# Attention ahead of an RWKV-style mix on one core: row maxima turned before the V product and the row sums, first scores right behind the sums

## What is computed

```
x = x + attn(layernorm(x))     # 8 heads of 64, softmax over 1024 keys, then W_out, layer norm, (y + x) / sqrt 2
x = x + mix(layernorm(x))      # r = sigmoid(xr W_r), k = xk W_k, out = r * (relu(k)^2 W_v)

qk  = x @ W_qk + b_qk          # q and k of every head, interleaved
v   = x @ W_v + b_v
sim = q k^T * 64^-0.5
o   = softmax(sim) v
```

## Time and profile before

| | |
|---|---|
| median of 3 runs | 2722.21 us |
| profiled execution, own time | 2721.03 us |
| its span | 2719.2 us |
| mean granted TensorE clock | 0.989 |
| TensorE (PE) busy | 2625.8 us, 97% |
| VectorE (DVE) busy | 1631.3 us, 60% |
| ScalarE (ACT) busy | 1290.6 us, 47% |
| GpSimd (POOL) busy | 1521.1 us, 56% |
| idle before ACT's exponentials (L623), ended by PE | 589.6 us |
| idle before DVE's maxima (L417), ended by PE | 543.4 us |

### The profile page before, as it was taken

How to read it: one execution, slowest core, us unless ns; L and a number is a source line. 1 busy time by engine, 2 the same in 40 slices (tenths; PEclk the granted TensorE clock), 3 DMA queues, 4 the chain that set the end, 5 groups by cost and what they waited for, 6 DMA issues and landing times. The chain is left out here.

```text
span 2719.2 us, 31997 instructions
## 1 busy us (share of the span) xinstructions
PE 2625.8 (97%) x11376; PEld 1782.0 (66%) x11376; DVE 1631.3 (60%) x2679; ACT 1290.6 (47%) x1833; POOL 1521.1 (56%) x819
## 2 busy tenths in 40 slices
PE   6999999999999999999999999999579999999999
PEld 5655656665565666556556666665358888888887
DVE  7555455456545545654554555455278787878785
ACT  3345346335534634553463455344245555555554
POOL 3576477567647756764775676577323333333333
PEclk9999999999999999999999999999779999999999
DMA  2222122122112212211221221122322222222220
GB/s 97 63 47 51 36 78 53 42 71 55 44 38 75 55 40 71 57 42 48 66 55 40 70 60 39 40 50 79 122 90 99 85 96 89 93 92 89 96 77 32
DMA packets 108410, 178.32 MB, mean 66 GB/s; under 512 B 22401, under 2 KB 22913, under 8 KB 108289
## 3 DMA queue, kind: packets, MB, share of 16 engines
q1 hardware_dynamic: 108288, 176.75, 22.5%
HBM read 92.02 MB, written 50.59 MB: 52 GB/s over the span
## 5 line engine op out<-in xcount | busy, mean ns | idle before, releaser
L417 DVE TENSOR_REDUCE half_max<-ps_max 128x1 f32<-128x512 f32 x1024 | 680.3, 687 | 549.7 <-PE ps_max L780 543.4
L324 POOL TENSOR_TENSOR acc<-acc,probs 128x1024 f32<-128x1024 f32 x384 | 914.0, 2380 | 157.5 <-ACT probs L623 109.2
L623 ACT ACTIVATE probs<-ps_st 128x1024 f32<-128x1024 f32 x512 | 522.0, 1023 | 591.8 <-PE ps_st L801 589.6
L812 PE MATMUL ps_o<-probs,v 128*64 128x512 f32 x2048 | 467.7, 598 | 0.0
L800 PE MATMUL ps_st<-qA,kA 128*128 128x512 f32 x1024 | 415.3, 406 | 13.9 <-DMA qB<-max_row 9.4
L801 PE MATMUL ps_st<-qB,kB 65*128 65x512 f32 x1024 | 408.2, 399 | 0.0
L780 PE MATMUL ps_max<-kA,qA 128*128 128x512 f32 x1024 | 386.8, 416 | 3.7 <-issue 1.4
L320 POOL TENSOR_TENSOR acc<-probs 128x1024 f32<-128x1024 f32 x64 | 152.8, 2387 | 287.6 <-ACT probs L623 287.6
L812 PEld LDWEIGHTS ps_o<-probs,v 128*64 128x64 f32 x2048 | 135.6, 136 | 265.4 <-issue 236.5
L780 PEld LDWEIGHTS ps_max<-kA,qA 128*128 128x128 f32 x1024 | 188.6, 188 | 138.6 <-issue 63.5
L800 PEld LDWEIGHTS ps_st<-qA,kA 128*128 128x128 f32 x1024 | 194.7, 190 | 82.3 <-ACT probs L623 32.7
(11 more groups left out here) (174 smaller groups left out, 4629.6 us busy)
## 6 DMA issues: line engine op xcount, KB each, us to landing
stage<-in_L_attn_x_dram SPq DMA_DIRECT2D x32, 512.0 KB, 5.8
qA<-qA SPq DMA_DIRECT2D x128, 128.0 KB, 2.3
kB<-kA SPq DMA_DIRECT2D x128, 128.0 KB, 2.4
o_hi_scratch<-spare SPq DMA_DIRECT2D x128, 128.0 KB, 2.3
o_lo_scratch<-oT SPq DMA_DIRECT2D x128, 128.0 KB, 2.4
o_hi<-o_hi_scratch SPq DMA_DIRECT2D x16, 1024.0 KB, 5.4
o_lo<-o_lo_scratch SPq DMA_DIRECT2D x16, 1024.0 KB, 7.7
xc<-in_L_attn_x_dram SPq DMA_DIRECT2D x16, 1024.0 KB, 5.2
```

Source lines behind the costliest of these rows:

```text
L324: pool.tensor_tensor(acc[:, :], acc[:, :], probs[:, j, :], ALU.add).then_inc(acc_done, 1)
L417: dve.tensor_reduce(half_max[:, r, kh:kh + 1], ps_max[(j + 1) % 2][:, :], AX_X, ALU.max).then_inc(max_done, 1)
L623: act.activation(probs[:, j, :], ps_st[j % 2][:, :], ACT.Exp).then_inc(exp_done, 1)
L812: ins = pe.matmul(ps_o[half * DH:(half + 1) * DH, :], v[:, j, hd * DH:(hd + 1) * DH], probs[:, j, half * HALF:(half + 1) * HALF], start=(j ...
```

## The change

Nothing is added to or taken from the arithmetic. Eight things are reordered or made to wait:

1. TensorE: `turn_max` stands ahead of `p_at_v(.., 4)` and `sum_rows` in every head.
2. TensorE, plain heads and head 0 of a batch: a new `front`. The first block of scores follows the sums at once, and blocks 1 to 3 and maxima products 0 to 4 are woven with the twelve products of the second q and k half, which was first before.
3. TensorE: the products of the other q and k half (`project_qk(b, h+2, 0, ..)`) stand at the end of the head, behind the last maxima products, which come in pairs (12, 13) and (14, 15) instead of one by one.
4. ScalarE: `store_max_row` comes ahead of `store_qk_hi(.., 0)`, `store_o` ahead of `store_sums`, and in plain heads two exponentials ahead of `store_qk_hi(.., 1)`.
5. SyncE: `place_max_row` comes ahead of `copy_qk(.., 0)`.
6. VectorE, plain heads: `invert_sums` comes ahead of the second conversion.
7. GpSimd, once at the start: `wv_lo` waits for VectorE's four `wqk_lo`.
8. The first maxima products, before head 0, are ordered like 3.

```diff
@@ sync
+                    place_max_row(b, h)
                     if has_next(b, h, 1, last):
                         copy_qk(b, h + 1, 0)
-                    place_max_row(b, h)
@@ gpsimd
                 pool.wait_ge(wv_hi_done, 1)
+                pool.wait_ge(wq_lo_done, KC)
                 pool.tensor_tensor(wv_lo[:, :, :], wv_raw, f32(wv_hi[:, :, :]), ALU.subtract).then_inc(wv_lo_done, 1)
@@ vector, plain_head
                     reduce_max(b, h + 1, 0, 3)
-                    store_qk_lo(b, h + 1, 1)
-                    reduce_max(b, h + 1, 3, 4)
                     if h >= 1:
                         invert_sums(b, h - 1)
-                    reduce_max(b, h + 1, 4, 16)
+                    store_qk_lo(b, h + 1, 1)
+                    reduce_max(b, h + 1, 3, 16)
@@ scalar, plain_head (the special heads alike, without the two exponentials in heads 6 and 7)
+                    store_max_row(b, h)
                     if more:
                         store_qk_hi(b, h + 1, 0)
-                    store_max_row(b, h)
                     if h >= 1:
+                        store_o(b, h - 1)
                         store_sums(b, h - 1)
-                        store_o(b, h - 1)
                     if h >= 2:
                         store_o_hi(b, h - 2)
+                    exponent(b, h, 0, 2)
                     if more:
                         store_qk_hi(b, h + 1, 1)
-                    exponent(b, h, 0, TT)
+                    exponent(b, h, 2, TT)
@@ tensor
                 def begin_head(b, h):
+                    turn_max(b, h)
                     if h >= 1:
                         p_at_v(b, h - 1, 4)
                         sum_rows(b, h - 1, 8 * b + h + 1)
-                    turn_max(b, h)
+                def front(b, h):
+                    begin_head(b, h)
+                    if h == 0:
+                        free_of_v(b, 3)
+                    scores(b, h, 0, 1)
+                    free_of_qk(b, h + 1, 0)
+                    project_qk(b, h + 1, 1, 0, 4)
+                    rows(b, h + 1, 0, 1)
+                    scores(b, h, 1, 2)
+                    project_qk(b, h + 1, 1, 4, 8)
+                    rows(b, h + 1, 1, 2)
+                    project_qk(b, h + 1, 1, 8, 12)
+                    rows(b, h + 1, 2, 3)
+                    scores(b, h, 2, 3)
+                    rows(b, h + 1, 3, 4)
+                    scores(b, h, 3, 4)
+                    rows(b, h + 1, 4, 5)
@@ tensor, plain_head behind the front
+                    scores(b, h, 4, 5)
+                    rows(b, h + 1, 5, 6)
                     if more:
                         free_of_qk(b, h + 1, 1)
                         project_qk(b, h + 2, 0, 0, 4)
+                    rows(b, h + 1, 6, 8)
+                    scores(b, h, 5, 6)
                     rows(b, h + 1, 8, 10)
                     p_at_v(b, h, 0)
                     rows(b, h + 1, 10, 12)
                     scores(b, h, 6, 7)
+                    rows(b, h + 1, 12, 14)
+                    scores(b, h, 7, 8)
+                    rows(b, h + 1, 14, 16)
+                    if more:
+                        project_qk(b, h + 2, 0, 4, 12)
@@ tensor, late_v_head behind the front
+                    rows(b, h + 1, 5, 7)
                     free_of_qk(b, h + 1, 1)
                     project_v(bb, 4)
...
-                    rows(b, h + 1, 14, 15)
+                    rows(b, h + 1, 14, 16)
                     project_qk(b, h + 2, 0, 0, 12)
-                    rows(b, h + 1, 15, 16)
@@ tensor, turning_head, its end
-                    rows(b, h + 1, 12, 13)
+                    rows(b, h + 1, 12, 14)
                     project_qk(b, h + 2, 0, 4, 8)
-                    rows(b, h + 1, 13, 14)
+                    rows(b, h + 1, 14, 16)
                     project_qk(b, h + 2, 0, 8, 12)
-                    rows(b, h + 1, 14, 16)
```

More of the change, by code:

```diff
@@ L842, in _ @@
                 free_of_qk(0, 0, 0)
-                for i in range(3):
-                    project_qk(0, 1, 0, 4 * i, 4 * i + 4)
-                    rows(0, 0, 12 + i, 13 + i)
+                rows(0, 0, 12, 13)
+                project_qk(0, 1, 0, 0, 4)
+                rows(0, 0, 13, 15)
+                project_qk(0, 1, 0, 4, 8)
                 rows(0, 0, 15, 16)
+                project_qk(0, 1, 0, 8, 12)
                 def begin_head(b, h):
+                    turn_max(b, h)
                     if h >= 1:
@@ L863, in plain_head @@
                     rows(b, h + 1, 2, 3)
-                    scores(b, h, 0, 1)
+                    scores(b, h, 2, 3)
                     rows(b, h + 1, 3, 4)
-                    scores(b, h, 1, 3)
-                    rows(b, h + 1, 4, 6)
                     scores(b, h, 3, 4)
-                    rows(b, h + 1, 6, 8)
+                    rows(b, h + 1, 4, 5)
+                def plain_head(b, h, last):
+                    front(b, h)
+                    scores(b, h, 4, 5)
+                    rows(b, h + 1, 5, 6)
                     more = not (last and h == HEADS - 2)
@@ L873, in plain_head @@
                         project_qk(b, h + 2, 0, 0, 4)
-                    scores(b, h, 4, 5)
+                    rows(b, h + 1, 6, 8)
+                    scores(b, h, 5, 6)
                     rows(b, h + 1, 8, 10)
-                    scores(b, h, 5, 6)
                     p_at_v(b, h, 0)
@@ L879, in plain_head @@
                     scores(b, h, 6, 7)
-                    rows(b, h + 1, 12, 13)
+                    rows(b, h + 1, 12, 14)
+                    scores(b, h, 7, 8)
+                    rows(b, h + 1, 14, 16)
                     if more:
-                        project_qk(b, h + 2, 0, 4, 8)
-                    rows(b, h + 1, 13, 14)
-                    scores(b, h, 7, 8)
-                    rows(b, h + 1, 14, 15)
-                    if more:
-                        project_qk(b, h + 2, 0, 8, 12)
-                    rows(b, h + 1, 15, 16)
+                        project_qk(b, h + 2, 0, 4, 12)
                 def late_v_head(b, h):
                     bb = b + h // HEADS
-                    begin_head(b, h)
-                    free_of_qk(b, h + 1, 0)
-                    project_qk(b, h + 1, 1, 0, 4)
-                    rows(b, h + 1, 0, 1)
-                    project_qk(b, h + 1, 1, 4, 8)
-                    rows(b, h + 1, 1, 2)
-                    project_qk(b, h + 1, 1, 8, 12)
-                    rows(b, h + 1, 2, 3)
-                    if h == 0:
-                        free_of_v(0, 3)
-                    scores(b, h, 0, 1)
-                    rows(b, h + 1, 3, 4)
-                    scores(b, h, 1, 3)
-                    rows(b, h + 1, 4, 6)
-                    scores(b, h, 3, 4)
-                    rows(b, h + 1, 6, 7)
+                    front(b, h)
+                    rows(b, h + 1, 5, 7)
                     free_of_qk(b, h + 1, 1)
```

23 lines of the change are left out of this document (10 added, 13 removed).

## The result

The changed kernel takes 2735.89 us (median of 6 runs, 2735.04 to 2738.88) against 2722.49 before (6 runs, 2721.84 to 2724.07): ratio 1.005, 95% interval 1.0037 to 1.0063, so it is slower, by 0.5%. The profiled executions are 2735.82 and 2721.03 us of own time, spans 2734.0 and 2719.2.

What follows compares the result with a forecast made beforehand. TensorE, busy 97% of the span, was taken to bound the kernel. Terms +5.2, +12.6, +4.2, -6.7, -4.3, +2.8 and -6.0 sum to +7.8 on 2721.0, 2728.8; with 1.2 for the median 2730.0 us, range 2715 to 2741.

Steps and rivals of the forecast that it cites:

- The rule for a stop: TensorE: a product counts from 0.16 us after the end of what it waits for, such as a VectorE maximum.
- X + 2.75 and X + 4.12: Earliest times of products 4 and 5, X being the second half's last projection; in plain heads stops of 0.20 and 0.21.
- the pairs at products 9 and 13: Plain heads: product 9 waits 0.26 for maximum 7, product 13, right behind 12, waits 0.25 for maximum 11.
- The rival of a gap that closes: Second conversion's chain is shorter, so stops at products 4 and 5 vanish in 40 heads: faster, 2707 us; chance 0.1.
- Head 0 of a batch: Batches 1 to 7: products 4, 5, 6 in a row wait 0.20, 1.14, 0.73; +1.8 each, +12.6 in all.
- the misread 0.97 above: Head 0: maximum 4 was said to end 0.97 after maximum 3, making product 6 wait 0.73.
- worth nothing by itself ... I charge 0.02: Plain heads: moving the transposition ahead of the V product overlaps what follows and costs only 0.02.
- Head 6 and head 7: Batches 0 to 6: head 6 +0.6 each, +4.2, from product 15 and transposition waits; head 7 -0.95 each, -6.7.
- The last two heads: Program end, where sums wait for GpSimd: last head but one -1.7, last head -4.3, together -6.0.
- at its own pace: Last head but one: GpSimd's chain leaves TensorE free to reach the sums, so sums to sums falls 25.9 to 24.2.
- The start: Holding back wv_lo lets the 4.98 us wqk_lo conversion take 0.68: -4.3, all TensorE idle time; head 0 of batch 0 +2.8.
- the term of -3.9: The start's term instead of -4.3, if the q and k bias scaling waits for the held-back wv_lo until 29.0.

Runs made afterwards that it cites:

- plain_apart: Changed kernel, plain heads only: two projections between maxima products 6 and 7, one between 12 and 13; 2720.29 us, ratio 0.9991 to the kernel before.
- late_apart: Changed kernel with maxima products 5 and 6 of head 0 of each batch put into the first V projection, five products apart; 2726.79 us, ratio 1.0016.
- turn_inside: Changed kernel with the transposition of the maxima ahead of the last q and k projection, in plain heads and heads 0 and 7; 2739.19 us, ratio 1.0057.
- turn_amid: Changed kernel with the transposition behind the first two products of the V product's second half; 2755.6 us, ratio 1.0115.
- turn_behind: Changed kernel without item 1: transposition of the maxima put back behind the row sums; 2998.3 us in one execution.
- exp_behind: Changed kernel with ScalarE's exponentials 0 and 1 put back behind the second half's q and k conversion; 2876.86 us in one execution.
- combined: Changed kernel with the wait-removing edits together: earlier second-half projections, maxima products set apart in plain heads, head 0 and head 6; 2691.26 us, ratio 0.9887.

## Why the prediction was right, and where it was off

It forecast 2730.0 us, slower, in 2715 to 2741; the result is 2735.9. Between the two profiled executions it forecast +7.8, and they are 14.8 apart: 7.0 were missed.

- **The rule for a stop held.** 0.16 behind a maximum's end, X + 2.75 and X + 4.12 were right to 0.02. The stops in plain heads came at the places and with the sizes given, and plain_apart shows that the pairs at products 9 and 13 carry 0.47 of a head, where 0.51 was forecast. The rival of a gap that closes is out: X + 2.76 and 4.14 were measured.
- **Head 0 of a batch: right.** +1.7 a head against +1.8. The wait at product 6 was 0.58 instead of 0.73, the misread 0.97 above, 1.0 in seven heads. The seven were +13.6 all the same, because one of them has a stretch at half the granted clock (40.54 against 39.02), which is no term of the sum. That the total of this row came out near is in part luck. late_apart shows that the two waits in a row are the cause: set apart, they take 1.19 of the head with them.
- **The step that was mis-sized is "worth nothing by itself ... I charge 0.02"** for the transposition ahead of the V product. It costs 0.10: 0.23 and 0.20 around it, 0.43, against 0.33. Before, it had stood in the passage out of the full 32-bit sums, where it cost 0.01. The reason given, that the passage stays in either order, is true, and misses that the transposition hid in it. Some 0.08 more in 61 heads is 4.9 of the 7.0 missed. The rest is 1.5 for the stretch at half clock and 1.3 for the last head but one, less the 1.0 at product 6, and 0.3 in small terms. turn_inside and turn_amid show the price at two other places.
- **Head 6 and head 7:** +0.69 against +0.6, -0.81 against -0.95; 0.08 of each miss is the transposition; the other 0.06 in head 7 is open.
- **The last two heads:** the last had -4.3, as forecast. The last but one had -0.35 instead of -1.7. The step that failed there is that TensorE reaches the sums "at its own pace": this head lacks its twelve projections, so nothing stands between product 15 and the transposition, and that waits 1.36 for the join. The same wait was priced in head 6 and not looked for here.
- **The start: -1.3 against -1.5, in part by luck.** The first projection is at 24.08, 4.3 earlier, as forecast. But "all of it TensorE's idle time" isn't so: the thirteenth projection is at 28.89 against 32.65, 3.8 earlier, since eight distances between the first projections are 0.43 here, and six were before. And the granted clock did not halve in head 0, the bound that the prediction gave. In the trace of plain_apart, whose list is the same up to there, it is 0.89 over 45 to 60 us, and the first sum stands at 93.19 instead of 91.63: +0.3 and not -1.3.
- **What held up the conversion.** Before, the conversion of 4.98 ran beside `wv_lo` and ended at 28.24, 0.55 behind it; with `wv_lo` held back it takes 0.68. The one of 1.78 is there before and after. It runs beside GpSimd's `wqk_lo` (20.33, 1.84 long), which nothing holds back, and also ends 0.55 behind it. So three of the four take 0.68, and not all four. The Trainium skill (SBUF — State Buffer, Who interferes with whom) lets an instruction on VectorE with two SBUF inputs and one on GpSimd that reads SBUF exclude each other; by that rule, the trace agrees. The second half of that rule, for a plain scaling, no run here shows. The scaling ran at 23.85 for 0.15, ahead of `wv_lo` at 24.07, so nothing waited until 29.0 and the term of -3.9 is out.
- **What the change does, item by item.** Direct scores need both the early transposition (turn_behind, +262 us without) and the early exponentials (exp_behind, +141), each in one execution. The old stops they remove (0.83 in a plain head) are truly gone. What gives all of it back is 0.41 at products 4 and 5, which wait for the second conversion and the maximum behind it, 0.5 at the pairs, and 0.1 for the transposition. The pairs are separable: with them set apart a plain head is at 25.73, below the 25.99 before, and with all the edits of combined the whole is 1.1% below the kernel before. What items 4 to 6 are worth each, apart from the exponentials, no run shows.

## What to carry to other kernels

Where two buffers are passed between a producer of one step (0.23) and a consumer of three (0.69), count for every product how many steps it stands behind the one two before it. A pair in a row, or a small instruction in the consumer's list, was a stop here that was not made up later. Independent products belong between them, in ones and twos, and not all at the head's end. The price of a small instruction depends on the kind of its neighbours: measure the distances around it at the old and at the new place. And when the last turn of a loop lacks the work that fills a gap in the others, look again at each wait which that work covered.

## What the runs showed of the hardware that was not expected

- **Passages between kinds of product.** A full 32-bit product of 512 columns starts 0.43 behind another (3.49 for the eight from 858.51 to 862.00, with the slower second). The first of them starts 0.33 behind a product of the 0.23 kind, and the second 0.48 behind the first; what follows starts 0.53 behind the last one, and its own follower 0.34 later. The transposition of the maxima costs 0.10 among 0.23 products, 0.01 in the passage out of full 32-bit ones, and 0.35 amid them.
- **The granted clock halves behind stops.** Behind a stop of 2.4 us the granted clock was 0.57 over 4 us (turn_behind, 1007 to 1011), in most of its heads; in the changed kernel the same happened in one head 0 of seven (batch 4), behind its two stops of 1.14 and 0.58:

```profile
1021.00:1025.00 4.00, 4.00 (x12) 3.18 (x11) 0.89 (x2) 0.00 (x0) 2.37 (x1) 0.58 0.22 68
```

  It costs 1.5 us there. The same head 0, with the same stops, has it in one head of seven in the traces of the changed kernel and of plain_apart, and in two in that of turn_inside, in other batches each time; what decides it is open. At the start of the program it moves the first sum by 1.6 us between two traces of the same list (91.63 and 93.19). So a forecast of one execution of this kernel is uncertain by 1.5 us for each such stretch, whatever its terms.
- **Moving the transposition two products back** (turn_amid) came with the half clock in all seven heads 0 of its trace (40.8 each, of which 1.5 is that), behind the same two stops. No run tells why.
